# Turned rows of the router kept on chip for the shared expert, in the two mixture-of-experts stages of a perceiver kernel

## The reference, cut to what matters

```
def _L2_ffn_ref(x, router_w, experts_bias, w1, w3, w2, sw1, sw3, sw2):
    xf = x.reshape(-1, d)
    sg = jnp.einsum('td,sdh->tsh', xf, sw1)
    su = jnp.einsum('td,sdh->tsh', xf, sw3)
    shared_out = jnp.einsum('tsh,shd->td', jax.nn.silu(sg) * su, sw2)
    logits = xf @ router_w.T + experts_bias
    rw, sel = jax.lax.top_k(logits, K)
...
    moe_out = jnp.einsum('te,teh,ehd->td', cw, eo, w2)
    return (moe_out + shared_out).reshape(b, l, d)

def _L3_ffn_ref(x, router_w, router_bias, sw1, sw3, sw2, ew1, ew2):
    shared_out = jax.nn.silu(xf @ sw1) * (xf @ sw3) @ sw2
    s = jax.nn.sigmoid((xf @ router_w.T).astype(jnp.float32))
...
    h = jax.nn.gelu(jnp.einsum('nd,edh->neh', xf, ew1), approximate=False)
    return (shared_out + routed_out).reshape(B, T, C)
```

## Time and profile before

| | |
|---|---|
| median of 3 runs | 3566.3 us (3560.57 to 3572.57) |
| the profiled execution, its own time | 3571.8 us |
| its span from first to last instruction | 3570.0 us |
| TensorE busy | 3298.9 us, 92% of the span |
| VectorE, ScalarE, GpSimd busy | 2152.4, 1428.5, 1017.6 us |
| mean granted TensorE clock | 0.958 of full speed |
| stage l2f | about 2380 to 2760 us of the span |
| stage l3f | about 3329 to 3566 us of the span |

### The profile page before, as it was taken

One profiled execution on the slowest core, in us unless ns is written; L12 is line 12 of the kernel. 1 busy time (PEld: TensorE's weight loads), 2 busy tenths in 40 slices (PEclk: granted clock), 3 DMA queues, 4 the chain that ended last, 5 costly groups with the idle time before them and its releaser, 6 DMA issues. The chain is left out here.

```text
span 3570.0 us, 105629 instructions
## 1 busy us (share of the span) xinstructions
PE 3298.9 (92%) x39322; PEld 2646.9 (74%) x39322; DVE 2152.4 (60%) x7124; ACT 1428.5 (40%) x4209; POOL 1017.6 (29%) x1587
## 2 busy tenths in 40 slices
PE   8988889999986999999999999887999999998799
PEld 6767777777765888888877777774666788878576
DVE  3766225555656888889645555763334566558545
ACT  2334335555532333333245555541111455555222
POOL 0112113333342444445333333442110111112421
PEclk9999999999997999999999999978999999999799
DMA  6653334212103000000041111033112411110323
GB/s 208 216 175 154 102 94 108 61 56 56 64 1 140 3 3 3 2 3 2 2 99 43 40 47 46 2 111 124 46 47 72 87 38 38 41 34 2 108 79 114
DMA packets 149258, 238.26 MB, mean 67 GB/s; under 512 B 14456, under 2 KB 121720, under 8 KB 147176
## 3 DMA queue, kind: packets, MB, share of 16 engines
q1 hardware_dynamic: 138816, 203.16, 18.2%
q0 software_dynamic: 10176, 31.47, 3.1%
HBM read 213.61 MB, written 38.94 MB: 71 GB/s over the span
## 5 line engine op out<-in xcount | busy, mean ns | idle before, releaser
L3299 POOL TENSOR_TENSOR l1fu_second_weighed<-l1fu_second,l1fu_parts 128x256 bf16<-128x256 bf16 x384 | 278.7, 753 | 339.2 <-DVE l1fu_second L3540 332.3
L3351 PEld LDWEIGHTS l1fu_ps_u<-l1f_xnT_all,l1f_key_in 128*128 128x128 f32 x2048 | 252.0, 195 | 17.3 <-issue 11.0
L3351 PE MATMUL l1fu_ps_u<-l1f_xnT_all,l1f_key_in 128*128 (+1 forms) x2048 | 254.9, 278 | 8.6 <-issue 5.5
L3362 PE MATMUL l1fu_ps_y<-l1f_key_out,l1fu_units 128*128 128x256 f32 x1024 | 250.6, 389 | 2.0 <-DVE l1fu_units L3548 2.0
L3362 PEld LDWEIGHTS l1fu_ps_y<-l1f_key_out,l1fu_units 128*128 128x128 f32 x1024 | 185.7, 190 | 33.6 <-issue 6.2
L3413 ACT COPY l1fu_plane<-l1fu_ps_p 128x512 f32<-128x512 f32 x128 | 75.1, 586 | 250.4 <-PE l1fu_ps_p L3341 250.4
L3535 DVE TENSOR_TENSOR l1fu_first<-l1fu_index,l1fu_counted 128x1024 bf16<-128x1024 bf16 x128 | 166.8, 1303 | 12.8 <-PE l1fu_ps_p L3341 9.6
L3421 ACT ACTIVATE l1fu_units<-l1fu_ps_u 128x512 f32<-128x512 f32 x128 | 76.6, 598 | 151.9 <-PE l1fu_ps_y L3362 139.9
L1020 ACT ACTIVATE l3x_scores<-l3x_scores,l3x_minus_big 128x257 f32<-128x257 f32 x256 | 129.0, 511 | 2.3 <-DVE l3x_minus_big L1109 2.3
L1020 ACT ACTIVATE l1x_scores<-l1x_scores,l1x_minus_big 128x257 f32<-128x257 f32 x256 | 128.9, 511 | 2.1 <-DVE l1x_minus_big L1109 2.1
L1020 ACT ACTIVATE l2x_scores<-l2x_scores,l2x_minus_big 128x257 f32<-128x257 f32 x256 | 128.8, 511 | 2.1 <-DVE l2x_minus_big L1109 2.1
(11 more groups left out here) (743 smaller groups left out, 8383.6 us busy)
## 6 DMA issues: line engine op xcount, KB each, us to landing
rows_by_expert<-in_zeros_dram SPq DMA_DIRECT2D x1, 17544.0 KB
l0x_ctxT<-in_ctx_T_dram SPq DMA_DIRECT2D x32, 514.0 KB, 5.2
l0x_ctx_rows<-in_ctx_dram SPq DMA_DIRECT2D x64, 256.0 KB, 3.3
l0f_w<-in_L_ffn_w_dram SPq DMA_DIRECT2D x16, 1024.0 KB, 5.2
l1x_ctx_sb<-in_ctx_T_dram SPq DMA_DIRECT2D x64, 256.0 KB, 2.8
l2x_ctx_sb<-in_ctx_T_dram SPq DMA_DIRECT2D x64, 256.0 KB, 2.8
l3x_ctx_sb<-in_ctx_T_dram SPq DMA_DIRECT2D x64, 256.0 KB, 2.8
l1x_mask_raw<-in_mask_int_dram SPq DMA_DIRECT2D x16, 514.0 KB, 3.9
```

What stands on the lines that cost most here:

```text
L3299: last = nc.gpsimd.tensor_tensor(second_weighed[:, k % 2, part], second[:, k % 2], parts[:, 1 - par, part, TC * k:TC * k + TC].unsqueeze(2 ...
L3351: last = nc.tensor.matmul(ps_u[:, k % 2, j, :], key_in[:, c, JS * k + j, :], xnT_all[:, c, bass.ts(tile, P)], start=(c == 0), stop=(c == C ...
L3362: last = nc.tensor.matmul(ps_y, units[:, k, j, :], key_out[:, JS * k + j, :], start=(k + j == 0), stop=(k == K - 1 and j == JS - 1))
```

## The change

The stage gets a new buffer `xnT` with one slot of turned rows per tile: 12 slots in l2f (`KEPT = 12`), 16 in l3f. The router's turned rows of a tile below `KEPT` are stored there and stay. A shared block on such a tile has no `turn_rows` and no `keep_rowsT` any more; its `up` reads `xnT`. The other blocks (the 39 routed ones, and in l2f the shared ones on tiles 12 to 15) are turned as before; since the sequence now has holes, the two buffers of `ps_x` and `xsT` go round by the count of turned blocks (`turned_by`) and no longer by n.

```
+    KEPT = 12 if routed[-1] else NT
...
+        xnT = sb("xnT", [P, KEPT, C, P])
...
+        def is_kept(n):
+            return order[n][0] == "shared" and order[n][1] < KEPT
+
+        turned_blocks = [n for n in range(N) if not is_kept(n)]
+
+        def turned_by(n):
+            return sum(k < n for k in turned_blocks)
+
+        def normed_rowsT(i):
+            return xnT[:, i] if i < KEPT else xsT[:, i % 2]
+
+        def rowsT(n):
+            return xnT[:, order[n][1]] if is_kept(n) else xsT[:, turned_by(n) % 2]
...
-                sp.wait_ge(s["turned"], FIRST + b + 1)
+                sp.wait_ge(s["turned"], turned_by(FIRST + b + 1))
...
-                    last = nc.tensor.matmul(ps_logits[i % 2][:, 0:E], xsT[:, i % 2, c, :], rw[:, c, :], start=(c == 0),
+                    last = nc.tensor.matmul(ps_logits[i % 2][:, 0:E], normed_rowsT(i)[:, c, :], rw[:, c, :], start=(c == 0),
...
             def turn_rows(n):
+                if is_kept(n):
+                    return
...
+                m = turned_by(n)
...
-                pe.wait_ge(s["xsT_ready"], max(n - 1, 0)) if n > 1 else pe.wait_ge(s["xnT_ready"], NT)
+                if m > 1:
+                    pe.wait_ge(s["xsT_ready"], m - 1)
+                else:
+                    pe.wait_ge(s["xnT_ready"], NT)
...
-                pe.wait_ge(s["xsT_ready"], n + 1)
+                if is_kept(n):
+                    pe.wait_ge(s["xnT_ready"], order[n][1] + 1)
+                else:
+                    pe.wait_ge(s["xsT_ready"], turned_by(n) + 1)
...
-                        last = nc.tensor.matmul(dst[:, 0:w.hidden], xsT[:, n % 2, c, :],
+                        last = nc.tensor.matmul(dst[:, 0:w.hidden], rowsT(n)[:, c, :],
...
             def keep_rowsT(n):
-                act.wait_ge(s["turned"], n + 1)
-                after(act, s["gate_up_ready"], n - 1)
-                after(act, s["up_ready"], swiglu_blocks(n - 1))
+                if is_kept(n):
+                    return
+                m = turned_by(n)
+                act.wait_ge(s["turned"], m + 1)
+                if m > 1:
+                    read = turned_blocks[m - 2] + 1
+                    act.wait_ge(s["gate_up_ready"], read)
+                    act.wait_ge(s["up_ready"], swiglu_blocks(read))
+                else:
+                    act.wait_ge(s["logits_ready"], NT)
...
-            act.wait_ge(s["logits_ready"], NT)
             keep_rowsT(0)
```

More of the change, by code:

```diff
@@ L2725, in turn_rows @@
                     rows = xn_all[:, i, :]
-                pe.wait_ge(s["xsT_ready"], max(n - 1, 0)) if n > 1 else pe.wait_ge(s["xnT_ready"], NT)
+                if m > 1:
+                    pe.wait_ge(s["xsT_ready"], m - 1)
+                else:
+                    pe.wait_ge(s["xnT_ready"], NT)
                 for c in range(C):
-                    last = nc.tensor.transpose(ps_x[:, n % 2, c * P:c * P + P], rows[:, c * P:c * P + P], ident)
+                    last = nc.tensor.transpose(ps_x[:, m % 2, c * P:c * P + P], rows[:, c * P:c * P + P], ident)
                 last.then_inc(s["turned"], 1)
@@ L2806, in keep_xnT @@
                 after(act, s["logits_ready"], i - 1)
-                nc.scalar.copy(xsT[:, i % 2].rearrange("p c n -> p (c n)"), ps_x[:, i % 2, 0:D]).then_inc(
+                nc.scalar.copy(normed_rowsT(i).rearrange("p c n -> p (c n)"), ps_x[:, i % 2, 0:D]).then_inc(
                     s["xnT_ready"], 1)
@@ L2818, in keep_rowsT @@
             def keep_rowsT(n):
-                act.wait_ge(s["turned"], n + 1)
-                after(act, s["gate_up_ready"], n - 1)
-                after(act, s["up_ready"], swiglu_blocks(n - 1))
-                nc.scalar.copy(xsT[:, n % 2].rearrange("p c n -> p (c n)"), ps_x[:, n % 2, 0:D]).then_inc(
+                if is_kept(n):
[8 more added lines that the diff above has]
+                    act.wait_ge(s["logits_ready"], NT)
+                nc.scalar.copy(xsT[:, m % 2].rearrange("p c n -> p (c n)"), ps_x[:, m % 2, 0:D]).then_inc(
                     s["xsT_ready"], 1)
```

## The result

| | before | after |
|---|---|---|
| median, runs side by side | 3565.13 us (3558.72 to 3576.12, 10 runs) | 3550.96 us (3545.32 to 3559.55, 10 runs) |
| ratio, 95% interval | | 0.9957 (0.9944 to 0.9971) |
| the profiled execution, its span | 3570.0 us | 3553.5 us |
| mean granted TensorE clock | 0.958 | 0.959 |

The change saves about 15 us by the ratio, 14.2 by the medians.

A forecast was written before the change was run, and what follows sets the result against it. Up to block 4 VectorE and GpSimd's scatter chain bound each stage, behind it TensorE. Turns -3.9 and clock +0.2 made -3.7 us, 3566.3 to 3562.6 us (chance 0.65), range 3555 to 3568.5.

The forecast's parts named there:

- Turns behind the start of block 4: TensorE, 7 turns in l2f and 11 in l3f go where TensorE is the bound, 0.217 us each: 3.9 us saved.
- The clock: TensorE's cold start at block 4 may warm later after a longer wait: +0.1 us in each stage, +0.2 in all.
- a cold block 4 that takes over 6 us for gate and up: Sign that the forecast is wrong: TensorE's gate and up matmuls of block 4 at the lower clock exceed 6 us.
- Turns ahead of block 4: Ten turns of blocks 0 to 4, two stages, lie in TensorE's waits: costed at nothing, 2.2 us if uncovered.
- Block 4 still waits for 2455.90: TensorE in l2f: block 3's earlier gate gains nothing, since block 4 waits for VectorE's product of block 3, ending 2455.90.
- The first rival: Early chain shortens: earlier block 0 activation moves VectorE and the second train, 3.1 us a stage; -9.9 us, 3556.4; chance 0.15.
- a second train that starts sooner behind the first: Sign that the forecast is wrong: GpSimd's two scatter trains no longer keep the 5.4 us between them.
- Trains close up: Rival: GpSimd's trains join, VectorE stays held and the last eight scatters wait; about +4 us, 3570 us; chance 0.06.
- Turns hidden anyway: Rival: VectorE's 0.20 us limits the tail, or the cold start takes 1.8 us; about 0, 3566 us; chance 0.14.
- Late instruction loads: Rival: if holds were late instruction loads, shorter ScalarE and TensorE programs shift them several us either way, 3556 to 3570.

The follow-up runs named there:

- after_d: The changed kernel again, unaltered, as yardstick of a later session: 3547.27 us against 3558.08 us for the kernel before, ratio 0.9968.
- late_last8_c: Changed kernel, GpSimd's last eight scatters waiting for VectorE's table of blocks: 3534.91 us, 0.9914 of the kernel before; 0.9992 and 0.9987 on chips without holds.
- before_again: The kernel before, unchanged, profiled again on another chip: 3561.94 us (1 run), beside a median of 3563.82 us for the kernel before.
- dep_only_c: Kernel before, all turns and copies kept; only kept blocks' up projection reads xnT, not awaiting the copy: 1.0009 of the kernel before; 0.9994 twice without holds.
- the first pair: First profiled session of the kernel before and the unaltered changed kernel: medians 3565.13 and 3550.96 us, ratio 0.9957.

## Why the prediction was wrong

**Turns behind the start of block 4 (3.9 us): right in kind and nearly in size.** The slot is 0.21 us (5.81 to 5.60). From the product of block 3 to the last down projection l2f went from 302.28 to 300.68 (372.64 less 70.36, 367.51 less 66.83): -1.60 us, where 7 turns at 0.217 and +0.1 for the clock make -1.4. l3f went from 159.99 to 158.77, -1.22 us, where -2.3 was forecast. The missing 1.1 us are the clock. The runs without holds, where block 4 starts at full clock, give the turns alone: -1.53 and -2.2 us.

**The clock (+0.2): mis-sized in l3f.** TensorE's block 4 in l3f after the change, against the earlier trace rows:

```profile
3389.39 3.75 PE L2776 MATMUL l3f_ps_g<-l3fs_w_up,l3f_xnT 128*128 128x512 f32 x4 [2.84 <-DVE l3f_hidden L3038]
3392.94 2.87 PE L2776 MATMUL l3f_ps_u<-l3fs_w_up,l3f_xnT 128*128 128x512 f32 x4
3395.64 0.60 PE L2786 MATMUL l3f_ps_h<-const,l3f_hidden 128*128 128x128 f32 x4
```

Gate and up take 6.25 us up to the next instruction, so the sign "a cold block 4 that takes over 6 us for gate and up" came true. From block 4 to block 5 it took 8.42 us, 7.57 before, although a turn has gone: +1.07 with the turn at 0.22, more than the +0.8 that I had worked out as the upper bound for l3f and had not taken. In l2f the same stretch took 7.16 against 7.45, so the term is -0.07. A start at full clock makes the part behind block 3 in l3f 156.13 us (after_d, where TensorE had waited 1.80 us), and the slow one makes it 158.77. Waits of 2.83 and 2.84 us were followed by a start at the lower of the two levels, as the 3.00 us in the earlier trace rows were, but the length of the wait does not settle it: in late_last8_c a wait of 2.90 us ahead of block 4 in l2f was followed by a gate of 1.96 us. The Trainium skill warns in "TensorE: Matmul & The Clock Gate", Part 1, that the ramp varies from run to run. The trace agrees in part: the kernel before took 7.45 us for this stretch of l2f in one profile and 8.89 in the other, behind waits of 3.00 and 4.62 us, but the slow starts of the changed kernel lie close together, 7.16 to 7.37 us in l2f (four profiles) and 8.36 to 8.56 in l3f (three).

**Turns ahead of block 4 at nothing, "the cover is VectorE's wait behind the scatter": this is the step that failed.** I took the end of each hold as fixed by the end of GpSimd's train, since four waits ended 2.8 to 2.9 us behind one. After the change the same add comes 0.0 us behind the train's end in l2f and 2.87 us ahead of it in l3f. The reading of before was sound: the tie is there in all six stages of before, before_again and dep_only_c, at 2.73 to 2.88 us. Wrong was to take it over to the changed kernel. It holds VectorE only while turn and copy are exchanged for every block, and the change takes just that away. "Block 4 still waits for 2455.90" fell with it. So the early turns and copies were not worth their own slots (2.2 us at most by the prediction) but the part of the hold that hung on them. It was 3.5 and 6.4 us in the first pair. Over the four profiles of the changed kernel the product of block 3 comes at R + 65.0 and 63.9 on average, in the two of before at 70.0 and 70.2: 5.0 and 6.2 us, which with some 3 us behind it gives the 14.2 us of the medians. Why indirect DMAs hold VectorE and ScalarE at all, and why the exchange makes it longer, stays open.

**The first rival was nearest.** It had the early chain shorten by 3.1 us a stage, through an earlier activation, VectorE and the second train. The place was right, the size half of it, and the way was another: the activation did come earlier, by 4.3 and 6.4 us, but the product of block 0 by 1.4 and 2.2 only, and the second train starts only 0.64 us sooner in l2f (R + 40.59 and not 41.23). Most of the gain arises behind its start. I gave this rival 0.15, on the argument that both engines went on behind the train. The sign "a second train that starts sooner behind the first" came too (4.73 us behind it and not 5.38).

**Trains close up (+4 us): not in the first pair.** In after_d's l3f they came within 2.34 us and the stage was shorter, not longer. Where there are no holds they join and no hold follows. **Turns hidden anyway: no,** the tail shows their slot. **Late instruction loads:** the program shrank and the time fell, but no packet of the two instruction queues lies between 2424 and 2449 us in either profile, while the second hold ended at 2448.89 and 2446.12; so they don't explain it. In the first hold there is one such packet, between 2419 and 2424 us before the change, but dep_only, the same program, had holds on one chip and none on two others. The Trainium skill's rule in "Runtime: NRT & Kernel Launch" (Instruction fetch mechanics), that a crossing is mostly hidden, is not contradicted.

**The range** took in the scatter of the runs but treated the early part as fixed, and its lower end was 3555 where the changed kernel's median is 3551. On a chip without holds the forecast sum would probably have been about right (3.3 to 4.7 us by late_last8, which also starts its last eight scatters later). That would have been no proof of the cover: there the early part has no hold to be covered by.

## What to carry to other kernels

When a wait ends at the same distance behind some other engine's work four times in one record, that can be real and still be true of this kernel alone: before costing a saving at nothing, ask whether the change touches what ties the two together, and what it would be worth if the wait only starts earlier and keeps its length. Here the exchange of turn and copy during another engine's train of indirect DMAs cost far more than its instructions, and cutting the train in two (eight scatters, then eight more when the dependent chain is through) was worth about as much as the whole change, 13.3 us. Take such a measurement on more than one chip, since these 50 us were absent on some. And where runs scatter by 6 us, compare a stretch of the profile that the edit touches: the turns' 1.5 and 2.2 us could be read to some hundredths there.

## What the runs showed of the hardware that was not expected

- The same program runs in about 3514 us in some sessions and in 3558 to 3565 in others. The profiles differ by holds of VectorE and ScalarE during GpSimd's indirect DMAs. Three sessions had none (chips numbered 6 twice, 11), three and the first pair had them (12, 0, 8). The scatter itself takes 0.96 us with 0.30 us between in both. No wait of TensorE was found that outlasts what it waits for in this way. What differs between the chips is open.
- Under holds VectorE's longest wait beside or just behind a train of 16 scatters (20 us) was 4.2 to 11.0 us, and beside one of eight (10 us) in late_last8_c none was above 2.7 us; in after_d, where two trains of eight came about by themselves in l3f, there were two of 3.34 and 3.58 us.
- Under holds the end of the early part moves by up to 8 us between profiles of one kernel (R + 58.74 to 66.69 in l3f of the changed kernel), while the first train starts at R + 15.64 to 15.77 in all of them.
